# Attention A: the six operand transfers of a pair issued in one step of the SyncE queue

## The chip, the cores and the metric

The kernel runs on 1 core of one Trainium2 chip. The time is that of the device, in microseconds, from launch to end; several runs are given by their median. Times of the profile come from one profiled execution, whose own time is given beside its span.

## What is computed

The whole is x (4 batches, 2048 rows, 256 columns) through four residual parts: attention A, a feed-forward part, attention B, the same feed-forward part. The change touches attention A alone:

```python
q = heads(x @ Wq + bq); k = heads(x @ Wk + bk); val = heads(x @ Wv + bv)
pos = _sinusoid_pos_emb(S, D) @ Wp + bp
pos = pos.reshape(S, H, P).transpose(1, 0, 2)
content_score = jnp.einsum('bhsp,bhtp->bhst', q + u, k)
pos_score = jnp.einsum('bhsp,htp->bhst', q + v, pos)
pos_score = _relative_shift(pos_score)
score = (content_score + pos_score) / jnp.sqrt(jnp.float32(P))
weights = jax.nn.softmax(score, axis=-1)
out = jnp.einsum('bhst,bhtp->bhsp', weights, val)
```

There are 16 heads of 16 columns, and S is 2048. The relative shift moves each row of the position scores by another amount.

## The kernel before, in words

One loop runs over the four batches (one body per engine, POOL's at L1447), and in it the stages follow each other: projections, attention A, output projection, feed-forward, then the same with attention B. Between stages all engines meet.

Attention A works through 16 heads x 16 tiles of 128 query rows per batch, 1024 tiles in all. Each operand of a product is held as three bf16 parts of the float32 value, stacked in 96 partitions, so that one bf16 product gives the sum of the products of the parts. A tile passes through these stations:

- PE makes the position scores of a tile in four pieces of 512 columns and a tail of 128 (`rows_of` L587, `row_tail` L606). ACT and DVE copy them to `rel` (L721, L797, L803).
- SP writes `rel` (1088 KB) to memory, `rel_rows` (`write_rows`, L882 to L891), and three steps later reads the same rows back into `z`, each row shifted by its own amount (`read_ready` L861, `read_rows` L876 to L880). This is the relative shift.
- PE makes the content scores (`content` L615), DVE adds them to `z` and takes the maximum (L764), POOL subtracts it (L825).
- PE turns `z` by transposes (L631), ACT takes the exponential into `pT` (L726), PE multiplies by the values (L652), and DVE copies and divides.

`rel` and `z` are rings of four tiles. The stations are offset by fixed leads: at step s, position scores are made for tile s+9 (`R_LEAD`), the read into `z` is issued for tile s+6 (`Z_LEAD`), DVE adds the scores of tile s+4 (`C_LEAD`), PE turns tile s+2, and the values are applied to tile s+1. `in_order` (L564) runs the steps: 9 leading steps, then 64 steps (`G`, four heads) in a loop body written out in full that is passed three times, then the same 64 once more as the last group.

All DMAs of attention A are issued by SP, in this order in each step: wait until `z` has a free slot (turned by PE) and the written rows are in memory, issue the read of tile s+6; wait until the copies to `rel` are done, issue the write of tile s+9; then `next_heads` (L893). That last one brings in the operands of coming heads. A pair of operands (`qu` and `k` of the next head, or `qv` and `pos` of the head after it) is three groups (`GROUP`), of 192, 128 and 64 KB, each with one transfer for the one operand (`load_still`, L834) and one for the other (`load_moving`, L840), six in all and 768 KB. Before the change group i goes out at step 1 + 2i of a head for `qu`/`k`, and at step 8 + 2i for `qv`/`pos`. The values of the next head (`load_v`) go out at step 7. The two buffers of each operand alternate by head. PE waits for `qu`/`k` of the next head at step 12 (`qk_loaded`), and for `qv`/`pos` when it begins that head's position scores, nine steps before the head.

The first of each batch, `load_pair(...)` at the head of `sp_attn_a` and `second_head`, are outside the change.

Of the kernel before, what the change touches and what calls it, by code (L numbers as in the profile page):

```python
# [32 lines left out]
NT = S // P  # L33
# [19 lines left out]
GROUP = [(0, KROWS, 3), (1, 64, 2), (65, KROWS, 1)]  # L53
# [6 lines left out]
HB = 4  # L60
NB = 2
# [3 lines left out]
C_LEAD = 4  # L65
# [33 lines left out]
def program(nc, a, out, nb=4, nh=H):  # L99

    ctx = ExitStack()
    with ctx:
        def sb(name, shape, dt=F32):
            return ctx.enter_context(nc.sbuf_tensor(name, shape, dt))
# [4 lines left out]
        def sem(name):  # L109
            return ctx.enter_context(nc.semaphore(name))  # L110
# [3 lines left out]
        qu_d = nc.dram_tensor("qu_parts", (PARTS, H, HD, S), BF16).ap()  # L114
        qv_d = nc.dram_tensor("qv_parts", (PARTS, H, HD, S), BF16).ap()
        k_d = nc.dram_tensor("k_parts", (PARTS, H, HD, S), BF16).ap()
        pos_d = nc.dram_tensor("pos_parts", (PARTS, H, HD, S), BF16).ap()
# [7 lines left out]
        qv_s = [sb("qv_s0", [KROWS, S], BF16), sb("qv_s1", [KROWS, S], BF16)]  # L125
        pos_b = [sb("pos_s0", [KROWS, PAD + S], BF16), sb("pos_s1", [KROWS, PAD + S], BF16)]
        pos_s = [t[:, PAD:PAD + S] for t in pos_b]
# [42 lines left out]
        qu_s = [xnT_f[0:KROWS, qu_at:qu_at + S // 2].bitcast(BF16), qk2[:, 0:S]]  # L170
        k_s = [k_sb[:, :], qk2[:, S:2 * S]]
# [76 lines left out]
        AA = {n: sem("A_" + n) for n in names + ["sub_lo", "sub_hi"]}  # L248
# [6 lines left out]
        r_full = [sem(f"r_full{c}") for c in range(4)]  # L255
# [17 lines left out]
        def settle(e):  # L273

            e.sem_inc(waited, 1)
# [288 lines left out]
        def in_order(e, b, step):  # L564

            def counts(p):
                return Counts(*(e.snap(b * (nh // HB * per) + p * per)
                                for per in (G, G // OB, 16 * G // RING, HB // NB * QK_INC, HB // NB * 16)))

            with e.Fori(0, 1) as p:  # L570
                base = counts(p)
                for s in range(-R_LEAD, 0):
                    step(p, base, s, lambda n: n >= 0)
            with e.Fori(0, GROUPS - 1) as p:
                base = counts(p)
                for s in range(G):
                    step(p, base, s, lambda n: True)
            with e.Fori(GROUPS - 1, GROUPS) as p:
                base = counts(p)
                for s in range(G):  # L580
                    step(p, base, s, lambda n: n < G)

        def moved(base, n):

            return base.moves + 16 * (n // RING + 1)
# [243 lines left out]
        def load_group(e, q, k, q_src, k_src, h, i, done):  # L829

            load_still(e, q, q_src, h, i, done)
            load_moving(e, k, k_src, h, i, done)

        def load_still(e, q, q_src, h, i, done):  # L834

            first, last, reps = GROUP[i]
            e.dma_start(q[first:last:2, :], q_src[0:reps, bass.ds(h, 1), :, 0:S]
                        .rearrange("r a d s -> (a d) r s")).then_inc(done, 16)
# [7 lines left out]
        def load_pair(e, q, k, q_src, k_src, h, groups, done):  # L846

            for i in groups:
                load_group(e, q, k, q_src, k_src, h, i, done)

        def load_v(e, h, hd, done):
            e.dma_start(v_s[hd].rearrange("p t w -> p (t w)"),
                        v_d[bass.ds(h, 1)].rearrange("a p w -> (a p) w")).then_inc(done, 16)

        def sp_attn_a(e, b):

            load_pair(e, qu_s[0], k_s[0], qu_d, k_d, 0, range(len(GROUP)), AA["qk_loaded0"])

            def second_head(s):

                if s == -R_LEAD:  # L861
                    load_v(e, 0, 0, AA["v_loaded0"])
                elif s <= len(GROUP) - R_LEAD:
                    load_still(e, qv_s[1], qv_d, 1, s + R_LEAD - 1, qv_loaded[1])

            def read_ready(p, base, n, fresh):

                k = n % RING
                if not fresh:

                    e.wait_ge(t_full[3], e.snap(base.tiles + (n - RING + 1)))
                    settle(e)
                e.wait_ge(rel_out[k], e.snap(moved(base, n)))
                settle(e)

            def read_rows(n):  # L876

                k, hd, i0 = n % RING, n // NT % NB, n % NT * P
                shifted = bass.AP(tensor=rel_d.tensor, offset=hd * FLAT + i0 * W + P - 1, ap=[[W - 1, P], [1, S]])
                e.dma_start(z[:, k, :], shifted).then_inc(rel_in[k], 16)  # L880

            def write_rows(base, n):  # L882

                k, hd, i0 = n % RING, n // NT % NB, n % NT * P
                for c in (R_DVE, R_ACT[-1]):
                    e.wait_ge(r_copied[c], e.snap(base.tiles + (n + 1)))
                    settle(e)
                e.wait_ge(tail_copied, e.snap(base.tiles + (n + 1)))
                settle(e)
                there = bass.AP(tensor=rel_d.tensor, offset=hd * FLAT + i0 * W, ap=[[W, P], [1, W]])  # L890
                e.dma_start(there, rel[:, k, :]).then_inc(rel_out[k], 16)  # L891

            def next_heads(p, base, s, final):  # L893

                hd, at = s // NT, s % NT
                nxt = (hd + 1) % NB
                if at in (1, 3, 5) and not (final and hd + 1 >= HB):
                    if at == 1:
                        e.wait_ge(AA["hi_ready"], e.snap(base.tiles + hd * NT + C_LEAD))
                        settle(e)  # L900
                    load_pair(e, qu_s[nxt], k_s[nxt], qu_d, k_d, e.snap(p * HB + (hd + 1)), ((at - 1) // 2,),
                              AA[f"qk_loaded{nxt}"])
                if at == 7 and not (final and hd + 1 >= HB):
                    e.wait_ge(AA["pv_done"], e.snap(base.tiles + (hd * NT + V_LEAD)))
                    settle(e)
                    load_v(e, e.snap(p * HB + (hd + 1)), nxt, AA[f"v_loaded{nxt}"])
                if at in (8, 10, 12) and not (final and hd + 2 >= HB):
                    if at == 8:
                        e.wait_ge(r_full[2], e.snap(base.tiles + (hd + 1) * NT))
                        settle(e)  # L910
                    load_pair(e, qv_s[hd % NB], pos_s[hd % NB], qv_d, pos_d, e.snap(p * HB + (hd + 2)), ((at - 8) // 2,),
                              qv_loaded[hd % NB])

            def step(p, base, s, here):

                n, r = s + Z_LEAD, s + R_LEAD
                final = not here(G)
                if here(n):
                    read_ready(p, base, n, s < 0 and n < RING)
                if here(n):  # L920
                    read_rows(n)
                if here(r):
                    write_rows(base, r)
                if s >= 0:
                    next_heads(p, base, s, final)
                else:
                    second_head(s)

            in_order(e, b, step)
# [655 lines left out]
```

## Time and profile before

| what | value |
|---|---|
| median of 3 runs | 9964.28 us (9959.06 to 9972.98) |
| the profiled execution's own time | 9955.88 us |
| its span, from first to last instruction | 9954.1 us |
| PE busy | 8957.4 us, 90% |
| DVE, ACT, POOL busy | 61%, 56%, 28% |
| mean DMA rate over the span | 256 GB/s |
| DMA rate in attention A | about 400 GB/s |
| mean granted TensorE clock | 0.962 |

Attention A takes the parts of the profile in which the DMA rate is near 400 GB/s: some 1450 us in each of four batches. In the rows, a line such as L880 is a line of the kernel. PE is TensorE's products, PEld its loads of weights, DVE is VectorE, ACT ScalarE, POOL GpSimd, and SPq the DMAs that SyncE issues. DMA share is the busy share of the core's 16 DMA engines, as a mean over a stretch; since a packet that straddles the edge of a stretch is counted with one side, it can come out a little over 1.

### The profile page before, as it was taken

What the parts mean: (1) busy time and instruction counts of PE and PEld (TensorE: products, weight loads), DVE (VectorE), ACT (ScalarE), POOL (GpSimd) and SP (SyncE); (2) the same over time, 40 slices, a digit from 0 to 9 for tenths busy, and PEclk for the clock granted to TensorE, in tenths of its full rate; (3) what the DMA queues carried; (4) which work ended last, traced back from release to release, by engine and by line L of the source; (5) the groups of instructions that cost most, each with busy time, mean ns of one, the idle gap of its engine ahead of it and who ended that gap; (6) DMA issues with size and microseconds to landing.
All of it is one profiled execution on the core that took longest, in us unless ns stands there. A gap on an engine that the chain in (4) does not pass through costs nothing. (4 is left out here: it accounts for less than half of the span.)

```text
span 9954.1 us, 256407 instructions
## 1 busy us (share of the span) xinstructions
PE 8957.4 (90%) x91488; PEld 5840.8 (59%) x91488; DVE 6024.0 (61%) x12530; ACT 5585.1 (56%) x10811; POOL 2778.8 (28%) x2894
## 2 busy tenths in 40 slices
PE   6988999899899998989989999998998898999899
PEld 4666666445566666644556666664555666666455
DVE  4666664664466666467456666646745666663673
ACT  4666664454466666445456666634545666663454
POOL 3333332100333333210033333321003333332101
PEclk8999999899999999989989999998998999999899
DMA  8999994110799999321079999922108999992210
GB/s 320 399 390 392 405 399 164 68 33 26 286 404 395 397 395 401 146 71 34 24 305 403 398 397 406 402 111 73 34 24 335 397 401 392 404 402 89 74 35 24
DMA packets 440126, 2552.03 MB, mean 256 GB/s; under 512 B 60016, under 2 KB 90224, under 8 KB 176368
## 3 DMA queue, kind: packets, MB, share of 16 engines
q1 hardware_dynamic: 438768, 2534.40, 64.7%
q8 instruction: 794, 13.01, 0.5%
q14 instruction: 564, 4.62, 0.1%
HBM read 1284.53 MB, written 1248.85 MB: 255 GB/s over the span
## 5 line engine op out<-in xcount | busy, mean ns | idle before, releaser
L825 POOL TENSOR_SCALAR z<-z,nmax 128x1024 f32<-128x1024 f32 x2048 | 2270.3, 1120 | 3655.7 <-DVE nmax L774 3655.7
L764 DVE CUSTOM_DVE_ANT_0 z<-sc,z 128x1024 f32<-128x1024 f32 x2048 | 2496.0, 1219 | 1190.6 <-DMA z<-rel_rows 1179.9
L721 ACT ACTIVATE rel<-rg 128x512 f32<-128x512 f32 x3072 | 1721.8, 596 | 1594.4 <-PE rg L598 880.2
L726 ACT ACTIVATE pT<-rg 128x512 f32<-128x512 f32 x4096 | 2226.9, 595 | 519.9 <-PE rg L631 519.3
L631 PE MATMUL rg<-ident,z 128*128 128x128 f32 x16384 | 2186.8, 277 | 3.7 <-ACT pT L726 3.2
L631 PEld LDWEIGHTS rg<-ident,z 128*128 128x128 f32 x16384 | 1785.8, 143 | 504.1 <-issue 361.2
L1075 ACT ACTIVATE pT<-rg 128x512 f32<-128x512 f32 (+3 forms) x2560 | 1226.1, 531 | 829.7 <-PE rg L1007 498.7
L1091 DVE TENSOR_REDUCE mx_b<-sc 128x1 f32<-128x1024 f32 (+7 forms) x1024 | 1004.0, 991 | 471.3 <-PE sc L989 235.5
L652 PE MATMUL op<-pT,xnT 128*32 128x128 f32 x32768 | 1118.7, 278 | 4.8 <-DVE rel L803 4.0
L797 DVE COPY rel<-rg 128x512 f32<-128x512 f32 x1024 | 708.3, 692 | 454.6 <-PE rg L602 422.5
L984 PE MATMUL sc<-z 96*128 96x512 bf16 (+3 forms) x2560 | 765.6, 370 | 149.5 <-DMA z<-k_parts 74.2
L652 PEld LDWEIGHTS op<-pT,xnT 128*32 128x32 f32 x32768 | 840.3, 110 | 47.9 <-issue 5.7
L640 PE MATMUL op<-sel,po_sb 128*128 128x32 f32 x2048 | 396.5, 276 | 483.5 <-DVE rel L803 469.3
L598 PE MATMUL rg<-pos_s,qv_s 96*128 96x512 bf16 (+3 forms) x2560 | 786.6, 357 | 16.7 <-DVE rel L797 15.7
L1007 PE MATMUL rg<-z 99*128 99x512 bf16 (+3 forms) x2560 | 743.5, 357 | 43.5 <-issue 24.8
L602 PE MATMUL rg<-pos_s,qv_s 96*128 96x512 bf16 (+3 forms) x2304 | 639.6, 360 | 86.5 <-issue 43.0
L640 PEld LDWEIGHTS op<-sel,po_sb 128*128 128x128 f32 x2048 | 306.8, 189 | 663.2 <-DVE rel L803 420.0
L624 PE MATMUL sc<-k_sb,xnT 96*128 96x512 bf16 x2048 | 631.9, 391 | 20.8 <-DVE mlo L764 19.6
L624 PE MATMUL sc<-xnT 96*128 96x512 bf16 x2048 | 617.8, 383 | 7.1 <-DVE mlo L764 7.1
L1148 POOL CAST half_b<-mx_b 128x16 bf16<-128x16 f32 x64 | 12.6, 196 | 2012.2 <-DVE mx_b L1096 2012.2
L1022 PE MATMUL rg<-pT,xnT 128*32 128x128 f32 x10752 | 493.3, 279 | 0.0
L984 PEld LDWEIGHTS sc<-z 96*128 96x128 bf16 x2560 | 227.4, 100 | 420.4 <-DVE mx_b L1091 158.4
(115 smaller groups left out, 8871.8 us busy)
## 6 DMA issues: line engine op xcount, KB each, us to landing
rel_rows<-rel SPq DMA_DIRECT2D x1024, 1088.0 KB, 9.1
z<-rel_rows SPq DMA_DIRECT2D x1024, 1024.0 KB, 9.6
v_heads<-rel SPq DMA_DIRECT2D x8, 4096.0 KB, 14.2
xnT<-v_heads SPq DMA_DIRECT2D x128, 256.0 KB, 4.3
qu_parts<-z SPq DMA_DIRECT2D x36, 512.0 KB, 4.4
pos_s<-pos_parts SPq DMA_DIRECT2D x64, 192.0 KB, 9.4
qv_parts<-z SPq DMA_DIRECT2D x24, 512.0 KB, 6.7
k_parts<-z SPq DMA_DIRECT2D x24, 512.0 KB, 5.6
```

The costliest lines, as they stand in the source:

```text
L598: mm = e.matmul(rg[:, R_BANK[c], 0:edge], qv_s[hd][:, i0:i0 + P], pos_b[hd][:, j0:j0 + edge], start=True, stop=True)
L624: mm = e.matmul(sc[:, c, :], qu_s[hd % NB][:, i0:i0 + P], k_s[hd % NB][:, c * CH:(c + 1) * CH], start=True, stop=True)
L631: mm = e.transpose(rg[:, T_BANK[q], (j - 4 * q) * P:(j - 4 * q + 1) * P], z[:, n % RING, j * P:(j + 1) * P], ident[:, :])
L652: mm = e.matmul(po[32 * g:32 * g + 32, :], v_s[hd % NB][:, j, :], pT[:, n % 2, j * P:(j + 1) * P], start=j < 4, stop=j + 4 >= NT)
L721: e.activation(rel[:, r % RING, c * CH:(c + 1) * CH], rg[:, R_BANK[c], :], ACT.Copy).then_inc(r_copied[c], 1)
L726: e.activation(pT[:, t % 2, q * CH:(q + 1) * CH], rg[:, T_BANK[q], :], ACT.Exp, scale=SCALE).then_inc(p_ready[q], 1)
L764: e.tensor_tensor_reduce(out=zs, in0=scf[:, 2 * half * CH:2 * (half + 1) * CH], in1=zs, scale=1.0, scalar=-3.0e38, op0=ALU.add, op1=ALU.ma ...
L825: e.tensor_scalar(zs, zs, 1.0, nmax[:, n % 2:n % 2 + 1], ALU.mult, ALU.add).then_inc(AA[done], 1)
L984: mm = e.matmul(scf[:, 2 * half * CH + c0 - k0:2 * half * CH + c1 - k0], q_b[n % HB][0:KROWS, s * P:(s + 1) * P], k_b[n % HB][0:KROWS, c0:c1],
L1007: mm = e.matmul(bank[:, i0 * P:CH], k_b[n % HB][:, kb * P:(kb + 1) * P], q_b[n % HB][:, g * CH + i0 * P:(g + 1) * CH], start=True, stop=kb ...
L1075: e.activation(pT_b[:, i % PTS, i0 * P:CH], rg[:, i % 2, i0 * P:CH], ACT.Exp, scale=SCALE).then_inc(BB["exp_done"], 1)
L1091: e.tensor_reduce(into, scf[:, 2 * half * CH:2 * half * CH + k1 - k0], AX.X, ALU.max, negate=True).then_inc(BB["reduced"], 1)
```

## The change

The steps 3 and 5 no longer issue anything, and step 1 issues all three groups of `qu`/`k` behind its wait. The steps 10 and 12 no longer issue anything, and step 8 issues all three groups of `qv`/`pos` behind its wait. The conditions on the last heads of a batch are as they were. `GROUP` has three entries, so `range(len(GROUP))` is 0, 1, 2.

```diff
                 hd, at = s // NT, s % NT
                 nxt = (hd + 1) % NB
-                if at in (1, 3, 5) and not (final and hd + 1 >= HB):
-                    if at == 1:
-                        e.wait_ge(AA["hi_ready"], e.snap(base.tiles + hd * NT + C_LEAD))
-                        settle(e)
-                    load_pair(e, qu_s[nxt], k_s[nxt], qu_d, k_d, e.snap(p * HB + (hd + 1)), ((at - 1) // 2,),
+                if at == 1 and not (final and hd + 1 >= HB):
+                    e.wait_ge(AA["hi_ready"], e.snap(base.tiles + hd * NT + C_LEAD))
+                    settle(e)
+                    load_pair(e, qu_s[nxt], k_s[nxt], qu_d, k_d, e.snap(p * HB + (hd + 1)), range(len(GROUP)),
                               AA[f"qk_loaded{nxt}"])
...
-                if at in (8, 10, 12) and not (final and hd + 2 >= HB):
-                    if at == 8:
-                        e.wait_ge(r_full[2], e.snap(base.tiles + (hd + 1) * NT))
-                        settle(e)
-                    load_pair(e, qv_s[hd % NB], pos_s[hd % NB], qv_d, pos_d, e.snap(p * HB + (hd + 2)), ((at - 8) // 2,),
+                if at == 8 and not (final and hd + 2 >= HB):
+                    e.wait_ge(r_full[2], e.snap(base.tiles + (hd + 1) * NT))
+                    settle(e)
+                    load_pair(e, qv_s[hd % NB], pos_s[hd % NB], qv_d, pos_d, e.snap(p * HB + (hd + 2)), range(len(GROUP)),
                               qv_loaded[hd % NB])
```

## Rows read from the trace of the kernel before

**Rows 1.** The page: busy time and share by engine; then the DMA queue.

```profile
PE 8957.4 (90%) x91488; PEld 5840.8 (59%) x91488; DVE 6024.0 (61%) x12530; ACT 5585.1 (56%) x10811; POOL 2778.8 (28%) x2894
...
q1 hardware_dynamic: 438768, 2534.40, 64.7%
```

**Rows 2.** Stretches of 92 us: engines' busy time (instructions), clock, DMA share, GB/s.

```profile
461.00:553.00 92.00, 79.89 (x891) 56.94 (x892) 58.80 (x129) 55.02 (x104) 33.24 (x30) 0.93 0.96 374
...
829.00:921.00 92.00, 80.47 (x892) 57.06 (x884) 57.74 (x129) 55.35 (x104) 33.26 (x30) 0.94 0.95 375
...
737.00:829.00 92.00, 82.98 (x970) 58.93 (x974) 62.38 (x138) 59.76 (x114) 35.47 (x32) 1.00 1.01 404
...
8100.00:8192.00 92.00, 83.37 (x968) 59.24 (x966) 62.61 (x140) 60.24 (x115) 35.47 (x32) 1.00 1.01 405
```

**Rows 3.** DMA issues: count, size of each, median time from issue to landing.

```profile
rel_rows<-rel SPq DMA_DIRECT2D x1024, 1088.0 KB, 9.1
z<-rel_rows SPq DMA_DIRECT2D x1024, 1024.0 KB, 9.6
...
xnT<-v_heads SPq DMA_DIRECT2D x128, 256.0 KB, 4.3
...
pos_s<-pos_parts SPq DMA_DIRECT2D x64, 192.0 KB, 9.4
```

**Rows 4.** Waits: total us, times, longest.

```profile
DVE z L764 <- DMA z<-rel_rows: 1179.9, 951, 6.4
...
PE rg L602 <- DMA qv_s<-qv_parts: 42.9, 4, 10.7
```

**Rows 5.** SP's timeline around step 1 of a head: start, length, what.

```profile
1003.70 0.32 SPq L891 DMA_DIRECT2D rel_rows<-rel  x1
...
1008.61 0.32 SPq L891 DMA_DIRECT2D rel_rows<-rel  x1
1009.11 0.61 SPq L837 DMA_DIRECT2D xnT<-qu_parts  x1
1009.83 1.33 SPq L843 DMA_DIRECT2D k_sb<-k_parts  x1
1011.42 1.04 SPq L880 DMA_DIRECT2D z<-rel_rows  x1
1013.65 0.32 SPq L891 DMA_DIRECT2D rel_rows<-rel  x1
```

**Rows 6.** SP's timeline: the transfers of values, one head apart.

```profile
1042.92 0.35 SPq L852 DMA_DIRECT2D xnT<-v_heads  x1
...
1133.59 0.34 SPq L852 DMA_DIRECT2D xnT<-v_heads  x1
```

**Rows 7.** Short stretches, with columns as in rows 2: dips, a clock fall, a turn.

```profile
1015.00:1018.00 3.00, 2.96 (x47) 2.17 (x46) 2.67 (x9) 1.87 (x4) 0.57 (x1) 1.00 1.04 314
1023.00:1026.00 3.00, 2.90 (x37) 1.96 (x38) 1.49 (x4) 0.21 (x1) 1.49 (x2) 0.60 0.99 413
1027.00:1030.00 3.00, 3.00 (x32) 2.51 (x34) 2.65 (x5) 2.16 (x5) 0.00 (x0) 1.00 1.01 312
1030.00:1037.00 7.00, 7.00 (x97) 4.75 (x90) 5.11 (x13) 4.97 (x10) 3.44 (x4) 1.00 1.01 424
1038.00:1041.00 3.00, 3.00 (x49) 2.41 (x48) 2.65 (x7) 2.26 (x5) 0.24 (x1) 1.00 0.98 369
...
1055.00:1059.00 4.00, 2.42 (x41) 1.52 (x39) 3.11 (x8) 1.33 (x3) 0.65 (x1) 1.00 1.03 329
...
535.00:541.00 6.00, 6.00 (x57) 4.48 (x55) 2.73 (x8) 3.46 (x6) 1.71 (x2) 0.67 0.24 55
```

**Rows 8.** SP's issue instructions by line: ns min/median/max.

```profile
L837 SPq DMA_DIRECT2D xnT<-qu_parts x192: 538/581/2124, 121.7 to 8907.4; - x192
...
L843 SPq DMA_DIRECT2D k_sb<-k_parts x96: 535/1004/1587, 122.3 to 8814.9; - x96
```

**Rows 9.** SP's timeline: first and last of six transfers issued together.

```profile
121.71 0.57 SPq L837 DMA_DIRECT2D xnT<-qu_parts  x1
...
124.23 0.59 SPq L837 DMA_DIRECT2D xnT<-qu_parts  x1
124.86 1.12 SPq L843 DMA_DIRECT2D k_sb<-k_parts  x1
```

**Rows 10.** Time to landing: all reads (L880); then the writes (L891) of 925 to 1110 us.

```profile
DMA to landing us min/median/max: 4.7/9.6/15.0
...
DMA to landing us min/median/max: 7.7/9.0/11.1
```

**Rows 11.** DVE's timeline: a score and its wait, as idle time in brackets.

```profile
1021.41 1.23 DVE L764 CUSTOM_DVE_ANT_0 z<-sc,z 128x1024 f32<-128x1024 f32 x1 [2.68 <-DMA z<-rel_rows]
```

## The prediction

> **What bounds the kernel now.** I read the page first. PE is busy for 90% of the span and would be the first suspect, while the DMA queue's packets take 64.7% of it [rows 1]. The share is a mean over stages, so the next view is busy time by stretches, each 92 us long, inside Attention A. There the core's 16 DMA engines show a share of 1.01, at 404 or 405 GB/s, while PE has 8 to 9 us of 92 free [rows 2]. The one stretch below that (0.96) holds the turn from one group of four heads to the next: 6 us in which the DMA share is 0.24 and the granted clock is down [rows 2, 7]. It comes at two places of a batch (the stretch of the second is in [rows 2] too, 0.95) and no edit touches it. Attention A is therefore bound by what the DMA engines carry and how fast they do. The view of waits agrees: DVE waits 1179.9 us, in 951 places out of 1024 tiles, for the rows of `z` that come back from memory [rows 4].
>
> A sum for one head tests this. A tile writes 1088 KB and reads 1024 KB back, a head has 16 tiles, one 256 KB transfer of values, and two pairs of operands [rows 3]. In KB of 1024 bytes that is 34.60 MB, 0.26 MB, and 2 x 768 KB = 1.57 MB (a pair is twice 192, 128 and 64 KB). The rate in stretches that hold no operand transfer is 424 GB/s [rows 7]: 81.6 + 0.6 + 3.7 = 85.9 us. The rate isn't held while operands land: three stretches of 3 us, behind the steps 1, 3 and 5, show 314, 312 and 369 GB/s, and 4 us behind step 8 show 329 [rows 7]. Against 424 that is 3 x (1 - 314/424) = 0.78, then 0.79, 0.39 and, for step 8, 0.90 us lost. The three of one pair lose 1.96 us, two pairs 3.9 us. Together 89.8 us a head; measured between the transfers of values of two heads in a row: 90.67 us [rows 6]. So bytes and dips explain the head to within 1%, and hardly anything is left over for waits in which no data moves.
>
> **The change, part by part.** It concerns 29 pairs a batch (15 of `qu`/`k`, 14 of `qv`/`pos`), so 116 in the four batches. Every one of the six transfers still goes out, from the same queue, with the same sizes.
>
> (1) *What is removed.* Steps 3, 5, 10 and 12 lose their two transfers each. SP's issue time goes with them, 0.58 us for a `qu` transfer and 1.00 for a `k` transfer by the medians [rows 8], and a few register instructions. SP isn't on the path: it waits for the engines between any two transfers, so I take 0.
>
> (2) *What is added to steps 1 and 8.* SP now issues three times 0.58 + 1.00 = 4.7 us where it issued 1.6 us. Behind it in SP's order stand the read of the next tile (L880) and then the write of the next tile (L891). In the trace of step 1 the write goes out at 1008.61, the two transfers at 1009.11 and 1009.83, the next read at 1011.42 and the next write at 1013.65 [rows 5]. With 3.2 us more of issuing, the read leaves at about 1014.6 and the write at about 1015. The medians were taken with a full queue; the six at the head of a batch, one behind the other, took from 121.71 to 125.98, 4.3 us [rows 9]. So the burst is 4.3 to 4.7 us long, perhaps 6 if the slow ones (over 1.2 us, as at 1009.83) pile up. No wait is added: the wait for `hi_ready` stays at step 1 and that for `r_full` at step 8.
>
> Does the late read cost anything? Only if the DMA engines run out of work. When the write of step 1 goes out there are 9.0 us of work in front of its end, by the median time to landing [rows 10]. The burst brings 786 KB / 424 = 1.85 us and its dips, 1.96 us, so 3.8 us of work for 4.7 us of SP. 9.0 + 3.8 - 5.2 (from the write to the end of the burst) leaves 7.6 us in the queue when the read joins it. Cost 0 if the engines run level. Ends of the range: 0 and 1.5 us a burst, the latter if the engines that are ahead have half of that queue or less.
>
> (3) *The read lands later.* It stands behind 384 KB more than before: 0.93 us, and behind their dips, 1.2 us. DVE's score of that tile waits some 2 us longer than now, in one place of the head, and the two stalls behind steps 3 and 5 go. A present stall is 2.68 us long [rows 11], so the new one is perhaps 4 to 5 us. While DVE stands, its copies `rel<-op` are late and PE with them, but already issued behind the awaited read are a write, a read, a write and a read: 4.3 MB, 10 us of DMA work. Hidden, then, by a full queue. What is late next is unchanged: the DMA engines.
>
> (4) *PE's clock.* After the present stall the granted clock is 0.60 over 3 us, 0.5 in its middle, which is the 1.2 GHz level, and the DMA rate is still 413 GB/s at a share of 0.99 [rows 7]. A fall costs PE about 1.5 us. PE's own step is 4.91 us where nothing is late (writes at 1003.70 and 1008.61 [rows 5]), 78.6 us a head, against 90.67. PE has 12 us to spare per head. 0.
>
> (5) *The dips.* This is the one term with a size. They go with volume: 0.78 (384 KB), 0.79 (256 KB), 0.39 (128 KB). By proportion 768 KB in one piece lose 1.96 us, what they lose now: 0. Lower end: one piece loses no more than the largest seen, 0.90, and 1.06 us a pair are won. Upper end: twice the present loss, 1.96 us more, as twice the amount of such transfers is in flight together. The nearest rows are those for 384 and 128 KB, a factor of 3 in size and 2 in loss, so proportion or a little less; I take 0.
>
> (6) *When the operands are ready.* They land earlier than now. PE needs `qu` and `k` of the next head at step 12, `qv` and `pos` 15 steps after step 8. The view of waits has PE waiting for operands only once a batch, four times in all, in the leading steps [rows 4]: none elsewhere now, none after.
>
> Sum: 0 on 9955.88 us, the profiled execution's own time (span 9954.1, and 1.8 around it). The median of the three runs is 8.4 us above it, at 9964.28, so I forecast 9964.
>
> The prologue's rows also bear on a rule. Six transfers of 192 to 64 KB took SP 0.57 to 0.59 us each, the last 1.12 [rows 9], while 64 KB at 424 GB/s are moved in 0.15 us. The Trainium skill, page "DMA: Bandwidth & Descriptors", section "Issuing engines are not separate DMA queues", says that starting a transfer is usually small beside the transfer itself. By that rule SP's burst could never starve the engines and the second rival below would have no chance; for 64 KB the rows say otherwise, so it keeps one.
>
> **The rivals.**
>
> *No net change (0.50).* As summed. 9964, own range 9944 to 9984.
>
> *The dips merge (0.27), faster.* One piece passes each engine in one go, and the time in which one engine fetches operands while another fetches `z` may grow less than the volume. For it: 256 KB lost as much as 384 KB, so length is not all that counts. Against it: 128 KB lost just half. At most 1.06 x 116 = 123 us, 9841; half of that is 9903.
>
> *SP starves the DMA engines (0.21), slower.* The read and the write of the next step leave 3.2 and about 1.4 us late, and the engine that is furthest ahead has nothing. For it: the shortest time to landing of a read is 4.7 us where the median is 9.6 [rows 10], so the queue is not always deep, and SP's burst may be 6 us. Against it: the share is 1.01 now with pairs that hold SP for up to 2 us. It decides from the point where the burst outlasts the shortest engine's queue plus 3.8 us. 0.8 us a burst is 93 us: 10057; 0.2 to 1.5 us are 9987 to 10138.
>
> *PE becomes the bound (0.02), slower.* Longer stalls, more clock falls: to cost anything they must eat 12 us a head, eight falls. With one more microsecond per pair, 10080.
>
> That the change doesn't do what it says isn't likely: the order in which SP issues is written out in the program, and SP takes it as it stands.
>
> **How the numbers follow.** The likeliest is 9964. The range takes the first case whole, the second down to 9870 (0.8 us won per pair) and the third up to 10040 (0.65 us lost per burst); outside stay a quarter of the second and half of the slower ones, 0.19. A measurement of this kernel can tell about 0.2%, 20 us, from no change. Faster by more than that 0.27, within it 0.50, slower 0.23.
>
> **What would show it.** The SP timeline: six transfers in a row within 4.3 to 6 us in steps 1 and 8, the next read behind them. Stretches of 92 us: share still at 1.01 and near 404 GB/s; below 1.00 the starving is real. Stretches of 3 us: one dip of some 4 to 6 us per pair whose loss against 424 is 1.96 us; if it is 1 us, the second case holds. DVE's longest waits for `z` grow to 4 or 5 us and become fewer, with their total near 1180 us. The forecast is wrong if the total DMA time of a head moves by over 0.3 us, the sum's 20 us spread over its 64 heads.

## The result

The changed kernel takes 10,193.92 us (median; 10,180.15 to 10,199.54), the kernel before 9966.31 us in the same comparison: ratio 1.0227, interval 1.0214 to 1.0240. That is 228 us more, or 2.0 us for each of the 116 bursts. The forecast was no change, with a range that ended at 10,040.

The profiled execution's span is 10,189.5 us. DVE, ACT and POOL are busy within 21 us of [rows 1]. PE is busy for 119 us more with the same 91,488 products, as goes with the lower clock below. The rest of the 235 us by which the span is longer is time in which PE waits.

The page of the changed kernel, busy time and DMA queue, and its longest waits of DVE (the second answers [rows 4]):

```profile
PE 9076.4 (89%) x91488; PEld 5953.7 (58%) x91488; DVE 6044.8 (59%) x12530; ACT 5591.2 (55%) x10811; POOL 2787.3 (27%) x2894
...
q1 hardware_dynamic: 438768, 2534.40, 64.6%
```

```profile
DVE z L764 <- DMA z<-rel_rows: 1128.3, 740, 6.6
```

Stretches of 92 us, with the columns of [rows 2] (busy times of PE, PEld, DVE, ACT, POOL, then granted clock, DMA share, GB/s):

```profile
369.00:461.00 92.00, 80.45 (x912) 57.76 (x914) 59.35 (x132) 56.61 (x108) 33.37 (x30) 0.94 0.99 382
...
645.00:737.00 92.00, 78.83 (x888) 56.45 (x889) 58.17 (x129) 54.21 (x104) 33.35 (x30) 0.93 0.98 375
737.00:829.00 92.00, 82.47 (x950) 59.01 (x949) 61.05 (x136) 58.45 (x111) 34.79 (x32) 0.96 1.00 390
```

Where [rows 2] had 404 GB/s at a share of 1.01 and a clock of 1.00, there are 375 to 390 GB/s, a share of 0.98 to 1.00 and a clock of 0.93 to 0.96. So two things happened to the DMA engines: they stand still for 1 to 3% of the time, and while busy they carry 2 to 4% less (rate over share). A head takes 95.65 us between its transfers of values (991.04 to 1086.69), against 90.67 in [rows 6].

One burst, at step 8 of a head. First SP's timeline (answers [rows 5]):

```profile
995.63 0.32 SPq L891 DMA_DIRECT2D rel_rows<-rel  x1
996.22 0.60 SPq L837 DMA_DIRECT2D qv_s<-qv_parts  x1
...
1000.80 0.54 SPq L843 DMA_DIRECT2D pos_s<-pos_parts  x1
1001.53 0.43 SPq L880 DMA_DIRECT2D z<-rel_rows  x1
1002.29 0.33 SPq L891 DMA_DIRECT2D rel_rows<-rel  x1
1002.92 0.32 SPq L880 DMA_DIRECT2D z<-rel_rows  x1
1006.78 0.32 SPq L891 DMA_DIRECT2D rel_rows<-rel  x1
1009.09 0.32 SPq L880 DMA_DIRECT2D z<-rel_rows  x1
1017.55 0.32 SPq L891 DMA_DIRECT2D rel_rows<-rel  x1
1021.92 0.32 SPq L880 DMA_DIRECT2D z<-rel_rows  x1
```

The read goes out 5.9 us behind the write, where it was 2.8 us in [rows 5]. Then, from 1009.09 to 1017.55, SP issues nothing for 8.5 us. DVE's timeline for the tile of the late read, and PE's first product behind it (in brackets the idle time before, and what ended it):

```profile
1011.71 1.23 DVE L764 CUSTOM_DVE_ANT_0 z<-sc,z 128x1024 f32<-128x1024 f32 x1 [5.05 <-DMA z<-rel_rows]
```

```profile
1013.20 0.64 PE L640 MATMUL op<-sel,po_sb 128*128 128x32 f32 x2 [4.28 <-DVE rel L803]
```

And short stretches of the same place (answer [rows 7]):

```profile
998.00:1008.00 10.00, 8.93 (x110) 6.03 (x104) 5.54 (x13) 6.25 (x12) 4.45 (x4) 1.00 0.99 322
```

```profile
1009.00:1017.00 8.00, 3.80 (x39) 2.53 (x40) 3.40 (x9) 1.33 (x4) 2.20 (x2) 0.75 1.01 425
...
1013.00:1019.00 6.00, 5.80 (x46) 4.06 (x47) 3.55 (x9) 1.19 (x3) 2.22 (x2) 0.50 0.91 382
1017.00:1018.00 1.00, 1.00 (x5) 0.53 (x4) 0.69 (x1) 0.36 (x1) 0.02 (x1) 0.50 0.58 241
1021.00:1024.00 3.00, 3.00 (x47) 2.12 (x46) 2.14 (x5) 2.17 (x5) 1.49 (x2) 1.00 0.55 174
```

Read in order of time: operands and reads together run at 322 GB/s for 10 us. DVE waits 5.05 us for the late read, and PE stands 4.28 us. When PE goes on, its clock is at 0.50, the 1.2 GHz level, for 6 us, so that the copies on which the next write waits (ACT's, L721) come late. The queue behind the read holds until 1017; then the DMA share falls to 0.58, and between 1021 and 1024 to 0.55. There the engines stand. It comes at most bursts: DVE waits more than 3.5 us for `z` in 110 places of this trace, in 5 of the trace before.

Standing is only a part of the loss. Added up from the DMA packets of both traces, over 230 of the 256 tiles of each batch, attention A is 241 us longer. Some 100 us of it is time in which engines stand, and some 138 us is slower work (busy time beyond what the bytes need at 424 GB/s).

### The profile page after: what moved, and what is told of

It reads as the page before. It is cut to its first block and busy times, and to the rows that moved or that the text cites. A ratio compares the mean times of both kernels' runs of the same rounds, so it can differ in the third digit from the quotient of the medians.

```text
span 10189.5 us, 256407 instructions
## 1 busy us (share of the span) xinstructions
PE 9076.4 (89%) x91488; PEld 5953.7 (58%) x91488; DVE 6044.8 (59%) x12530; ACT 5591.2 (55%) x10811; POOL 2787.3 (27%) x2894
## 5 line engine op out<-in xcount | busy, mean ns | idle before, releaser
L721 ACT ACTIVATE rel<-rg 128x512 f32<-128x512 f32 x3072 | 1723.1, 596 | 1747.2 <-PE rg L598 969.3
L631 PE MATMUL rg<-ident,z 128*128 128x128 f32 x16384 | 2219.5, 280 | 3.7 <-ACT pT L726 3.2
L631 PEld LDWEIGHTS rg<-ident,z 128*128 128x128 f32 x16384 | 1829.9, 145 | 507.3 <-issue 289.9
L652 PE MATMUL op<-pT,xnT 128*32 128x128 f32 x32768 | 1187.8, 289 | 4.2 <-DVE rel L803 3.5
L652 PEld LDWEIGHTS op<-pT,xnT 128*32 128x32 f32 x32768 | 886.1, 115 | 55.3 <-issue 5.0
L598 PE MATMUL rg<-pos_s,qv_s 96*128 96x512 bf16 (+3 forms) x2560 | 815.2, 370 | 16.6 <-DVE rel L797 15.7
L602 PE MATMUL rg<-pos_s,qv_s 96*128 96x512 bf16 (+3 forms) x2304 | 669.6, 375 | 89.3 <-issue 45.8
L809 DVE COPY po_sb<-op 128x128 f32<-128x128 f32 x1024 | 298.5, 292 | 318.2 <-PE op L652 278.2
```

The costliest lines, as they stand in the source:

```text
L598: mm = e.matmul(rg[:, R_BANK[c], 0:edge], qv_s[hd][:, i0:i0 + P], pos_b[hd][:, j0:j0 + edge], start=True, stop=True)
L631: mm = e.transpose(rg[:, T_BANK[q], (j - 4 * q) * P:(j - 4 * q + 1) * P], z[:, n % RING, j * P:(j + 1) * P], ident[:, :])
L652: mm = e.matmul(po[32 * g:32 * g + 32, :], v_s[hd % NB][:, j, :], pT[:, n % 2, j * P:(j + 1) * P], start=j < 4, stop=j + 4 >= NT)
L721: e.activation(rel[:, r % RING, c * CH:(c + 1) * CH], rg[:, R_BANK[c], :], ACT.Copy).then_inc(r_copied[c], 1)
```

## The experiments

Three explanations were open. *Clock:* the single long stall throws PE to 1.2 GHz, and its lateness empties the queue. *Order:* 768 KB in the queue ahead of a read make the stall, whatever SP and the clock do. *Hold:* SP is busy with six issues and the next read leaves late. Every run below was measured beside the kernel before on the same chip. The ratio is to that, and so is every loss in us below: the medians of the kernel before lie between 9961 and 9978 us, so times of different runs aren't subtracted from each other.

**PE kept busy in the stall.** The changed kernel with products that nobody reads, in the two steps of the long stalls. The wait ahead of them only makes sure that their bank is free.

```diff
+                    if (at == 4 and not (final and hd + 1 >= HB)) or (at == 11 and not (final and hd + 2 >= HB)):
+                        e.wait_ge(p_ready[2], base.tiles + (t + 1))
+                        for _ in range(13):
+                            e.matmul(rg[:, T_BANK[2], 0:P], ident[:, :], ident[:, :], start=True, stop=True)
                 if here(s):
                     e.wait_ge(tail_copied, base.tiles + (r + 1 if here(r) else G))
```

> The changed kernel with 13 more products of the identity with itself on PE (some 280 ns each, 3.6 us), in steps 4 and 11 of each head that has a burst, ahead of the wait in which PE stood 4.3 us in the trace of after; their result is read by nobody. Theory 1 (clock): the loss arises because PE, after so long a stall, works at 1.2 GHz for some 6 us, is late with the next write and read, and the DMA queue drains. Then the granted clock stays near 1.0 and the time falls to 10,000 to 10,080 us. Theory 2 (order in the queue alone: the read that stands behind 768 KB lands late, and the stall itself empties the queue whatever the clock is): 10,190 us or more. Theory 3 (SP is held by six issues and is late with the next read and write): 10,190 us or more.

Measured: 10,100.47 us, ratio 1.0128 (1.0111 to 1.0145). The loss is 127 us instead of 228, so 100 us came back although PE does more work. That is a little short of the 10,000 to 10,080 that the clock alone would give. The same stretch of the second batch, for the kernel before, the changed kernel and this one:

```profile
2680.00:4030.00 1350.00, 1220.40 (x14080) 867.79 (x14081) 907.26 (x2003) 871.78 (x1646) 521.41 (x471) 0.98 1.00 399
```

```profile
2680.00:4030.00 1350.00, 1192.32 (x13270) 849.60 (x13269) 868.35 (x1905) 832.18 (x1567) 498.19 (x448) 0.94 0.99 384
```

```profile
2680.00:4030.00 1350.00, 1275.50 (x14504) 931.99 (x14502) 886.23 (x1958) 853.70 (x1612) 509.97 (x460) 0.99 1.00 390
```

From the changed kernel to this one the clock goes from 0.94 to 0.99, the share from 0.99 to 1.00, the rate from 384 to 390 GB/s. The products did not shorten the stalls: DVE still waits over 3.5 us in 105 places. The mean clock of the run is back at the 0.962 of the kernel before, and 127 us of loss are left.

A mean over the 116 bursts shows what the clock does and what it doesn't. Counted from the start of the write ahead of the burst, the DMA share of the changed kernel has two holes: 0.97, 0.95, 0.88 and 0.96 in the four microseconds from 5 to 9, and 0.85, 0.89 and 0.96 in the three from 25 to 28. With the products the first is the same (0.98, 0.96, 0.89, 0.96), and the second is gone (1.00 in all three). So the fall of the clock makes the second hole, as late writes; the first has another cause.

**The products' own price.** The same products in the kernel before.

> The kernel before with the same 13 idle products in steps 4 and 11 as in the run that kept PE busy in the changed kernel: what those products cost by themselves. PE has some 12 us a head to spare, so by theory 1 they cost little, 9,960 to 10,010 us. If they cost 9,966 + 116 x 1 us or more, the 10,100 us of the changed kernel with them holds some cost of the products, and the clock's part is larger than the 93 us that they won.

Measured: 10,030.04 us, ratio 1.0049 (1.0032 to 1.0065), 52 us above its own reference and above the 10,010 I had expected at most. They aren't free where no long stall covers them. With the products on both sides the bursts cost 127 - 52 = 75 us in all instead of 228. So the clock accounts for 100 us at least, and for up to some 150 us if the products cost as much in the changed kernel as here, which the stall that covers them there makes doubtful.

**SP held, nearly without bytes.** The kernel before, plus four transfers of 3 KB behind those of steps 1 and 8. They copy part of an input into a tile that nobody reads. Ahead of the loop stands a wait for the four transfers of the place before.

```diff
+            def tiny_loads(base, hd, k):
...
+                for i in range(4):
+                    e.dma_start(tiny[0:KROWS:2, i, :], a["embT"][0:48, i * 16:(i + 1) * 16]
+                                .rearrange("(r d) s -> d r s", r=3)).then_inc(tiny_in, 16)
...
+                if at in (1, 8):
+                    tiny_loads(base, hd, int(at == 8))
```

> The kernel before, with four more transfers of 3 KB each (48 rows of 64 bytes, into a tile that nobody reads) behind those of steps 1 and 8: SP is held about as long as in the burst (4 x 0.55 us more), but only 12 KB join the queue. Theory 3 (SP held): 10,100 to 10,200 us. Theories 1 and 2: within 20 us of the kernel before, 9,966.

Measured: 10,149.03 us, ratio 1.0179 (1.0162 to 1.0196): 176 us for 128 places, 1.4 us each, with 12 KB more. A hold makes a loss of this size without the bytes of the burst. In the mean over its 116 places with a pair, the first hole is deeper than in the changed kernel (0.95, 0.74, 0.76 and 0.94 from 5 to 9 us behind the write), and there is no second one. SP's timeline and the stretches behind it:

```profile
1042.03 0.32 SPq L893 DMA_DIRECT2D rel_rows<-rel  x1
1042.53 0.61 SPq L839 DMA_DIRECT2D xnT<-qu_parts  x1
1043.24 1.11 SPq L845 DMA_DIRECT2D k_sb<-k_parts  x1
1044.54 3.72 SPq L900 DMA_DIRECT2D tiny<-in_embT  x4
1048.53 0.36 SPq L882 DMA_DIRECT2D z<-rel_rows  x1
```

```profile
1040.00:1047.00 7.00, 7.00 (x86) 4.69 (x79) 5.01 (x13) 4.79 (x9) 3.56 (x4) 1.00 1.01 423
...
1048.00:1051.00 3.00, 1.31 (x12) 0.96 (x10) 1.57 (x4) 1.92 (x4) 0.00 (x0) 1.00 0.79 204
1052.00:1054.00 2.00, 2.00 (x19) 0.80 (x10) 0.97 (x6) 1.00 (x2) 1.48 (x2) 0.53 0.94 236
```

The write left at 1042.03, the pair by 1044.35, and the rate, 423 GB/s until 1047, is 204 at a share of 0.79 from 1048 on. The queue ran low some 6 us behind that write, with 384 KB of operands to carry as well. Median times to landing of 9.0 and 9.6 us [rows 10] had looked like 9 us of stock. That time ends with the last of the 16 engines. The semaphore events of the trace have one report for each engine: for the write of 1042.03 the first came at 1047.15, 5.1 us after its issue, twelve by 1048.86, the last at 1051.59, after 9.6 us. So some engines were out of that write's work 4 us before the others. It is so in the kernel before too: over its 1024 writes the median of the first report is 5.4 us after issue, that of the last 9.1.

**Half the hold.** Two such transfers in place of four.

> As the run that holds SP alone, with two 3 KB transfers in place of four: SP's hold in steps 1 and 8 is about 3.5 us instead of 5 to 5.5. If the loss has a threshold near the length of the engines' queue: little is left, 9,970 to 10,000 us. If it is proportional to the hold: half of 176 us, 10,055 us.

Measured: 10,080.67 us, ratio 1.0105 (1.0089 to 1.0121): 111 us, 0.87 us a place, above both forecasts. A threshold near 5.5 us is out. Two issues cost more than half of what four do (0.87 and 1.4 us); a lower threshold stays possible, and the run in two steps below bears on it.

**The hold where SP waits anyway.** The four transfers behind the read of steps 2 and 9, ahead of its write.

```diff
                 if here(n):
                     read_rows(n)
+                if s >= 0 and s % NT in (2, 9):
+                    tiny_loads(base, s // NT, int(s % NT == 9))
                 if here(r):
                     write_rows(base, r)
```

> The run that holds SP alone with four 3 KB transfers, with these moved behind the read of steps 2 and 9, where SP waits for some 2.3 us anyway before it can issue the write. If a hold costs by the time by which the next read is held back: nearly nothing, 9,966 to 10,000 us. If a hold costs wherever it is (work of the four transfers in the queues, whatever their size): 10,149 us as before.

Measured: 9994.21 us, ratio 1.0018 (1.0008 to 1.0028), 20 us in place of 176. The transfers are the same, and hold SP for 2.9 us here and 3.7 us there:

```profile
1048.38 1.13 SPq L882 DMA_DIRECT2D z<-rel_rows  x1
1049.70 2.90 SPq L900 DMA_DIRECT2D tiny<-in_embT  x4
1052.93 0.33 SPq L893 DMA_DIRECT2D rel_rows<-rel  x1
```

So it isn't the work of those transfers in the queues; it is mainly the time by which the next read is held back.

**The hold with PE kept busy.**

> The run that holds SP alone (10,149 us) with the 13 idle products of PE in steps 4 and 11. The stall that follows the hold is shorter there (2.5 us in two steps, seen in its trace) and its place is the steps 2 and 3, so the products don't cover it. If the products help by the clock during the stall alone: no gain, 10,150 to 10,200 us. If they help in another way, by holding PE back: a gain as in the changed kernel, about 10,055 us.

Measured: 10,137.85 us, ratio 1.0169 (1.0154 to 1.0185), against 1.0179 without the products: 168 us of loss in place of 176, 12 us below the 10,150 of no gain. My reason was wrong, though. The products did keep the clock up: its mean over the run is 0.965, against 0.946 without them and 0.962 in the kernel before. The loss stayed even so. As the products cost 52 us in the kernel before, some gain by the clock may hide in it, but at least some 116 us (168 - 52) of what a hold costs need no fall of the clock. That the run without products has no second hole says the same.

**The burst behind the read.** The changed kernel, with its six transfers between the read and the write of steps 2 and 9 (`bursts` holds the two `load_pair` blocks of the change, with `at == 2` and `at == 9`).

```diff
                 if here(n):
                     read_rows(n)
+                if s >= 0:
+                    bursts(p, base, s, final)
                 if here(r):
                     write_rows(base, r)
```

> The changed kernel with the burst moved behind the read of the next step (between the read and the write of steps 2 and 9). The read that was late is now ahead of the 768 KB in the queue, and SP is not held before it. Theory 3 (SP held before the read): most of the loss goes, 9,970 to 10,050 us. Theory 2 (order in the queue): the next write and the read after it are behind the burst in its place, the stall moves on by one tile and has nearly its size: 10,120 to 10,200 us. Theory 1: as theory 2, since the stall is as long.

Measured: 10,071.74 us, ratio 1.0101 (1.0084 to 1.0118). The loss is 99 us; 129 of the 228 us came back. That is more than order alone would give, and less than hold alone: between the two expectations. The edit takes two things from ahead of the read, the hold and the 768 KB, and doesn't tell them apart. The write behind the burst is still late. It leaves at 1028.95, 5.7 us behind the read, where it is 2.6 us in the kernel before (1006.01 to 1008.61):

```profile
1023.27 0.32 SPq L880 DMA_DIRECT2D z<-rel_rows  x1
1023.77 0.83 SPq L837 DMA_DIRECT2D xnT<-qu_parts  x1
...
1028.95 0.33 SPq L891 DMA_DIRECT2D rel_rows<-rel  x1
```

**The same with PE kept busy.** Eight products in each of the steps 4, 5, 11 and 12.

> The changed kernel with the burst behind the read of the next step (alone 10,072 us) and with 8 idle products of PE in each of the steps 4, 5, 11 and 12, where that run's stalls lie. If hold and clock are two causes that add up: 10,072 - 94 is 9,978, and with what the products cost by themselves (up to 60 us) 9,978 to 10,040 us. If the clock costs only behind the one long stall that the hold makes: no gain, 10,072 us or more.

Measured: 10,045.25 us, ratio 1.0069 (1.0047 to 1.0092). The loss is 72 us. Each cure alone won 129 and 100 us, together they win 156. They overlap: a shorter stall is probably also one behind which the clock falls less, which no run shows by itself. Of the 72 us that stay with both, the products' own price is a part.

**The burst around the read.** Group 0 behind the write of step 1 (8), groups 1 and 2 behind the read of step 2 (9).

> The changed kernel with the six transfers split within one step's length: group 0 (two transfers) behind the write of step 1 as before, groups 1 and 2 (four) behind the read of step 2, ahead of its write; the same at steps 8 and 9. SP is never held for more than about 3 us at a time and the next read is held back by 1.6 us as in the kernel before, but 768 KB still join the queue within one step. If the loss is from SP's hold ahead of the read: below the 10,072 us of the burst behind the read, 9,970 to 10,040 us. If it is from 768 KB within one step: 10,072 or more, up to 10,190.

Measured: 10,056.30 us, ratio 1.0079 (1.0062 to 1.0096), a loss of 79 us. The interval overlaps that of the burst behind the read (99 us), and the time is above the 9970 to 10,040 of a pure hold ahead of the read. The four 3 KB transfers in the same place lost 20 us with about the same time from read to write (median 4.1 us, 4.2 here), so 768 KB within a step's length cost something in both placements tried.

**One burst of the two.** Only `qu`/`k` together, `qv`/`pos` in three steps.

> The kernel before with the burst at step 1 only (60 of the 116 bursts); qv and pos go out in three steps as before. If each burst costs by itself (228 us / 116 = 2.0 us): 9,966 + 118 = 10,084 us. If it is the second burst that meets a queue not yet refilled after the first, clearly less than 10,084, down to 9,966.

Measured: 10,072.27 us, ratio 1.0098 (1.0081 to 1.0115): 99 us for 60 bursts, 1.65 us each. A burst costs by itself. For the other 56, those of `qv`/`pos`, 228 - 99 = 129 us are left, 2.3 us each; why they cost more wasn't tried.

**Two steps.** Group 0 in step 1 (8), groups 1 and 2 in step 3 (10).

```diff
-                if at in (1, 3, 5) and not (final and hd + 1 >= HB):
+                if at in (1, 3) and not (final and hd + 1 >= HB):
...
-..., ((at - 1) // 2,), ...
+..., ((0,), (1, 2))[(at - 1) // 2], ...
```

> The kernel before with the groups 1 and 2 together in step 3 (and step 10), group 0 alone in step 1 (8): 384 KB and 384 KB. SP is held for 1.6 us and then 3.2 us. If the loss grows from the point at which the hold outlasts the engines' queue (some 5.5 us by the trace of the run that holds SP alone): little, 9,966 to 10,010 us. If it is proportional to the time by which the read is held back beyond 1.6 us (3.2 us more cost 2.0 us in the burst): 116 x 1.0 us, 10,080 us.

Measured: 9997.02 us, ratio 1.0018 (1.0008 to 1.0028). 20 us, 0.17 us a place, for four transfers at once with 384 KB. Set beside the other runs in which SP is held ahead of a read, this gives a curve. The third column is the median time from the write to the next read, over all such places in SP's timeline:

| run | operands at the place | write to read | loss, us a place |
|---|---|---|---|
| before, a pair | 128 to 384 KB | 2.5 us | 0 by definition |
| two steps, four transfers | 384 KB | 3.9 us | 0.17 |
| half the hold | 384 KB | 4.6 us | 0.87 |
| SP held | 384 KB | 5.8 us | 1.4 |
| changed | 768 KB | 6.2 us | 2.0 |

With the same 384 KB, a read 1.4 us later costs almost nothing, and the next 0.7 us cost 0.7. So there is a soft threshold, near 4 us from write to read, where I had looked for one near 5.5. (The step isn't quite the same: two steps issues its four in steps 3 and 10, and leaves 5 and 12 empty.)

**Six steps.** One transfer per step, in steps 1 to 6 and 8 to 13.

> The kernel before with one transfer per step: qu and k in steps 1 to 6, qv and pos in steps 8 to 13. SP is held for 0.6 to 1 us at a time and never has more than 192 KB ahead of a read. If already the pairs of before cost something by hold and stall: faster than before, 9,850 to 9,950 us. If before holds nothing back and only bytes and their dips count: 9,966 within 20 us.

Measured: 9952.68 us, ratio 0.9976 (0.9965 to 0.9988). Faster than before by 24 us, and just short of the 9850 to 9950 that I had hoped for.

**Six steps, behind the read.** The same, between the read and the write.

> One transfer per step (steps 1 to 6 and 8 to 13) as in the run that was faster than before, but behind the step's read and ahead of its write, where SP waits for some 2.3 us anyway. If the short holds of 0.6 to 1 us ahead of the next read still cost something: below 9,950 us by 10 us or more. If not: within 15 us of 9,953.

Measured: 9913.74 us, ratio 0.9939 (0.9926 to 0.9953). This is the fastest of all, 56 us below the kernel before. Its second batch, beside the 399 GB/s of the kernel before in the same stretch (shown above):

```profile
2680.00:4030.00 1350.00, 1236.10 (x14266) 875.02 (x14268) 917.57 (x2025) 884.74 (x1672) 530.53 (x478) 0.99 1.00 403
```

**Pairs behind the read.** The kernel before with its pairs in the same steps, behind the read in place of the write.

> The kernel before with its pairs in the same steps (1, 3, 5 and 8, 10, 12), but each pair behind the step's read and ahead of its write, where SP waits for some 2.3 us anyway. Nothing else differs. If it is the hold ahead of a read that costs, the pairs of before (some 1.6 us each) pay it too, and this is faster than before: 9,900 to 9,945 us. If only transfers finer than a pair help: 9,966 within 20 us.

Measured: 9976.70 us, ratio 1.0017 (1.0008 to 1.0026), 16 us slower than its own reference and within the 20 us of no gain; a faster kernel had been the point of the run. The place behind the read won nothing for pairs, and 0.4% for single transfers. So the 0.6% isn't the hold ahead of the read alone. It takes both, single transfers and that place. The packets say where the gain is: added up as above, the fastest run has 67 us less of slower work than the kernel before, and no less idle time. Why the engines work faster there is open.

## Why the prediction was wrong

*What bounds attention A* held in the main: bytes, rate and share explain the head. But PE isn't far behind the DMA engines, since 3.6 us more of its work in two steps of a head cost 52 us in the kernel before. Wrong was to take a share of 1.01 as a sign of a deep queue. It says that the engines are busy, not for how long they would stay so.

*Step (2), SP's hold.* The size was right: 5.1 us of SP for the six (996.22 to 1001.34), and a read that leaves 3 us later (5.9 us behind its write instead of 2.8). The price of 0 was the step that failed; a burst cost 2.0 us, and a hold with 12 KB in place of half the operands cost 1.4. The 0 rested on "9.0 us of work" in the queue, taken from the time to landing. That is the time of the engine furthest behind; the one furthest ahead had finished a write after 5.4 us in the median of the kernel before. I had asked whether the engines run level, and took it that they do. In the run that holds SP, the rate fell some 6 us behind the last large write, which itself landed after 9.6 us. The rival that starved the DMA engines had the right mechanism. Its 0.8 us a burst should have been 2.0, beyond its upper end of 1.5, and its threshold (the shortest time to landing, 4.7 us, plus 3.8) was too high: the loss sets in near 4 us from write to read.

*Step (3), the stall.* "Perhaps 4 to 5 us" came out as 5.05: 2.4 us more than 2.68, for the 2.1 us that the 384 KB and their dips were to add. The stalls became fewer (740 waits in place of 951), and their total, 1128 us, stayed near the 1180 forecast. But the 10 us of work behind the awaited read were counted from its issue. At 1011.71, when it had landed, 5 us were left: the share falls at 1017.

*Step (4), the clock.* The stall of 5 us brought 6 us at 1.2 GHz, where 2.7 us had brought 3 [rows 7, 11]. I had compared PE's loss with 12 us to spare in a head ([rows 2] give 8 to 9 in 92). The spare time isn't there in the 10 us behind the stall, in which the next write and read have to leave. With PE kept busy 100 us come back at least. I gave a rival of this kind 0.02, and only for stalls that eat a whole head's spare time.

*Step (5), the dips.* 10 us at 322 GB/s lose 10 x (1 - 322/424) = 2.4 us, against 1.96 for three dips now. In the mean over all bursts (5 to 14 us behind the write) it is 2.1 us for a burst and 0.75 for a pair, so three pairs lose no less and the term of 0 held. What had no term is the slower work outside the dips: the 138 us above must be nearly all of that kind. Some 0.5 us a burst of it lie at the second hole, from 24 to 30 us behind the write; the rest isn't located.

*The rival in which dips merge* did not show. *The parts together:* what stands ahead of the read, hold and bytes (129 us by moving the burst behind it), and the clock (100 us) overlap, 156 us together; some 72 us remain for 768 KB within one step and for the products' own price, which these runs don't separate.

## What to carry to other kernels

Where the DMA engines are the bound and one queue carries both the stream and its occasional extras, the extras belong one by one in the places where the issuing engine waits anyway, behind the transfer that others will wait for. In this kernel that gave 0.6%, and pairs in the same place gave nothing. A busy share of 1 is no reserve, and a time to landing isn't stock: ask how soon the first engine runs dry (its report is in the semaphore events), and test it by holding the issuing engine with transfers of a few KB. Slack of an engine over a whole loop can't be set against its lateness in the few microseconds in which it feeds the bound.

## What the runs showed of the hardware

- SP took 3.72 us to issue four transfers of 12 KB in all, and 5.1 us for six with 768 KB, but 0.32 us for one write of 1088 KB: an issue isn't priced by its bytes.
- The 16 engines don't finish a transfer together. In the kernel before, the first of them reported its part of a 1088 KB write 5.4 us after the issue, the last 9.1 us after it (medians of 1024 writes); for the reads of 1024 KB it was 6.0 and 9.6 us. The time to landing is the last one's.
- Idle time of 4.28 us of PE was followed by 6 us at 1.2 GHz. In the kernel before, 2.10 us were enough for a fall of 3 us, the clock being 0.50 from 1024 to 1027:

```profile
1023.10 0.38 PE L640 MATMUL op<-sel,po_sb 128*128 128x32 f32 x2 [2.10 <-DVE rel L803]
```

- Behind a drained queue the DMA engines were slow even as the last operands had landed: 236 GB/s at a share of 0.94 (1052 to 1054 us of the run that holds SP; the last report of its operand transfers is at 1052.63).
- In the dips it is the reads of `z` that slow down. Sorted by size, a read packet (8192 bytes) took 315 ns on average from 1030 to 1037 us in the kernel before, 464 ns from 1015 to 1018, 488 ns in the burst (998 to 1008), and 543 ns in the stretch of the bullet above. A write packet (8704 bytes) took 328 to 352 ns in all four. What slows the reads wasn't tried.
